# Up's and gate's last 64-row products issued as a pair on the two halves of TensorE's rows, gate's weight stack turned over

## What is computed

```python
up = jax.nn.silu(jnp.einsum('td,edh->teh', xt, Wu) + bu)
gt = jnp.einsum('td,edh->teh', xt, Wg) + bg
act = up * gt * w_full[:, :, None]
y = jnp.einsum('teh,ehd->td', act, Wd) + w_full @ bd
sh = jax.nn.silu(xt @ sWu + sbu) * (xt @ sWg + sbg)
y = y + sh @ sWd + sbd
```

## Time and profile before

| what | value |
|---|---|
| runs | 437.08, 439.56, 439.49 us, median 439.49 |
| profiled execution | 437.12 us, its span 435.3 us |
| granted TensorE clock, mean | 0.998 |
| PE busy | 422.8 us, 97% of the span, 2425 matmuls |
| PEld busy | 358.3 us, 82% |
| DVE busy | 309.1 us, 71% |
| ACT busy | 221.3 us, 51% |
| POOL busy | 99.4 us, 23% |

### The profile page before, as it was taken

How to read it: one execution, slowest core, us unless ns; L and a number is a source line. 1 busy time by engine, 2 the same in 40 slices (tenths; PEclk the granted TensorE clock), 3 DMA queues, 4 the chain that set the end, 5 groups by cost and what they waited for, 6 DMA issues and landing times.

```text
span 435.3 us, 7041 instructions
## 1 busy us (share of the span) xinstructions
PE 422.8 (97%) x2425; PEld 358.3 (82%) x2425; DVE 309.1 (71%) x966; ACT 221.3 (51%) x642; POOL 99.4 (23%) x143
## 2 busy tenths in 40 slices
PE   8999999999999999999999999999999999999995
PEld 7787679877799766997767987887888888889994
DVE  4888865487654796626989659888668688566564
ACT  1667666265672366923661356773444633434432
POOL 4131122132122222120041527985301100000000
PEclk9999999999999999999999999999999999999999
DMA  5979999999999999997650016222043220333300
GB/s 164 310 279 196 208 214 213 214 213 213 213 213 213 214 213 213 211 213 166 246 199 2 1 41 232 80 50 68 5 137 106 68 71 23 105 87 86 86 23 36
DMA packets 20997, 63.60 MB, mean 146 GB/s; under 512 B 2572, under 2 KB 10964, under 8 KB 20578
## 3 DMA queue, kind: packets, MB, share of 16 engines
q0 software_dynamic: 7552, 39.39, 42.9%
q1 hardware_dynamic: 12546, 22.68, 17.5%
q10 hardware_dynamic: 864, 1.09, 0.8%
HBM read 61.88 MB, written 1.27 MB: 145 GB/s over the span
## 4 chain that ended last, share of the span: by engine, by line
PE 51%; DMA 33%; DVE 8%; ACT 4%; issue 2%; SPq 1%; POOL 1%; ACTq 0%; DVEq 0%
DMA area_w<-in_L_attn_wte_dram 27%; PE bank L911 8%; PE bank L995 4%; PE bank L997 4%; PE bank L998 4%; PE bank L996 4%; PE bank L999 4%; DMA area_t<-in_L_attn_W_o_dram 3%; PE bank L1034 2%; PE bank L1043 2%; PE bank L1044 2%; PE bank L1035 2%; PE bank L1036 2%; PE bank L857 2%; DMA lnw<-in_L_attn_ln_w_dram 1%
## 5 line engine op out<-in xcount | busy, mean ns | idle before, releaser
L579 ACT ACTIVATE area_p<-area_p,nmax 128x128 f32<-128x128 f32 x96 | 37.4, 390 | 72.1 <-DVE nmax L1184 72.1
L911 PE MATMUL bank<-area_t,area_o 128*128 128x192 f32 (+1 forms) x432 | 72.3, 327 | 0.0
L911 PEld LDWEIGHTS bank<-area_t,area_o 128*128 128x128 f32 (+1 forms) x432 | 69.8, 182 | 0.6 <-issue 0.6
L650 ACT ACTIVATE area_p_r<-area_b 128x484 fp32r<-128x484 f32 (+1 forms) x51 | 30.6, 601 | 78.0 <-DVE area_b L1295 77.9
L471 POOL DMA_DIRECT2D area_w<-in_L_attn_wte_dram x26 | 31.1, 1196 | 129.2 <-DMA area_w<-in_L_attn_wte_dram 129.2
L857 PE MATMUL bank<-area_p,xn 128*128 128x356 f32 x96 | 39.7, 495 | 0.0
L1281 DVE SCALAR_TENSOR_TENSOR area_b<-bank,area_w 128x484 f32<-128x484 f32 (+1 forms) x36 | 23.4, 650 | 21.5 <-ACT bank L677 16.6
L602 ACT ACTIVATE area_b<-xb,w 64x192 f32<-64x192 f32 x96 | 38.1, 444 | 0.8
L1182 DVE CUSTOM_DVE_ANT_0 area_p<-bank,cmask 128x128 f32<-128x128 f32 x96 | 23.9, 286 | 12.6 <-PE bank L810 12.5
L799 PE MATMUL bank<-area_a,xa 128*128 128x256 f32 x96 | 29.1, 384 | 0.5 <-DVE area_a L1172 0.4
L521 POOL TENSOR_TENSOR area_b_r<-area_b,area_p_r 128x484 fp32r<-128x484 f32 x17 | 21.8, 1280 | 28.6 <-ACT area_p_r L650 28.6
(11 more groups left out here) (269 smaller groups left out, 1059.4 us busy)
## 6 DMA issues: line engine op xcount, KB each, us to landing
area_w<-in_L_attn_wte_dram POOLq DMA_DIRECT2D x28, 1344.0 KB, 12.6
area_w<-gate_rows SPq DMA_DIRECT2D x24, 242.0 KB, 3.2
area_k<-in_experts_dram SPq DMA_DIRECT2D x8, 353.0 KB, 5.8
area_w<-gate_rows SPq DMA_DIRECT2D x12, 228.0 KB, 3.2
area_a<-in_experts_dram SPq DMA_DIRECT2D x6, 353.0 KB, 5.5
area_b<-gate_rows SPq DMA_DIRECT2D x8, 242.0 KB, 3.2
area_t<-in_L_attn_W_o_dram SPq DMA_DIRECT2D x1, 1728.0 KB, 11.1
area_o<-in_x_dram SPq DMA_DIRECT2D x4, 384.0 KB, 6.1
```

The costliest lines, as they stand in the source:

```text
L579: act.activation(pm[:, sl, n, :], pm[:, sl, n, :], ACT.Exp, scale=-1.0, bias=nmax[:, sl, n:n + 1], accum_out=psums[:, sl, n:n + 1])
L650: act.activation(hid_high[:, sl, 0:w], hidT[:, sl, 0:w], ACT.Copy).then_inc(hid_high_ready, 1)
L911: last = pe.matmul(o, oT[:, c, at:at + n], woT[:, c, :], start=(c == 0), stop=(c == NCH - 1))
```

## The change

`products` issues four matmuls and no longer the fifth. A new function `half_rows(n)` is called at the end of `gate_of(n)` and issues two matmuls of 64 rows: up's high weights (rows 0 to 63 of its stack) with rows 0 to 63 of `xbl`, and gate's high weights with rows 64 to 127 of `xbl`. For that gate's stack is turned over: low rest in rows 0 to 63, high part in rows 64 to 127. `upper` and `sign` get a second column for gate, and ACT's and DVE's instruction for the stack becomes two, one for up and one for gate. `up_ready` is now raised by up's half-row matmul, which stands behind gate's four. The product of low weights with low activations of the 64 features is no longer computed (for the other 128 features it never was).

```diff
+            for c in range(2):
+                own.mark(pool.affine_select(out=upper[:, c:c + 1], in_=upper[:, c:c + 1], compare_op=ALU.is_gt, fill=1.0 - c,
...
+                own.mark(pool.affine_select(out=sign[:, c:c + 1], in_=sign[:, c:c + 1], compare_op=ALU.is_gt, fill=2.0 * c - 1.0,
...
-                act.activation(signed, wb(e), ACT.Copy, scale=sign[:, 0:1]).then_inc(wh_ready, 1)
+                act.activation(signed[:, 0], wb(e)[:, 0], ACT.Copy, scale=sign[:, 0:1])
+                act.activation(signed[:, 1], wb(e)[:, 1], ACT.Copy, scale=sign[:, 1:2]).then_inc(wh_ready, 1)
...
                 pe.matmul(o, both, xbh[:, p, 0:w], start=False, stop=False)
-                return pe.matmul(o, both, xbl[:, p, 0:w], start=False, stop=True)
+
+            def half_rows(n):
+
+                sl, g, e = n % 2, n // STEPS, n % STEPS
+                w, p = WIDE[g], g % 2
+                pe.matmul(bank[sl][:, 0:w], wbs(e)[0:64, 0], xbl[0:64, p, 0:w], start=False, stop=True).then_inc(up_ready, 1)
+                pe.matmul(bank[2 + sl][:, 0:w], wbs(e)[64:P, 1], xbl[64:P, p, 0:w], start=False, stop=True).then_inc(gt_ready, 1)
...
-                products(bank[sl], 0, g, e).then_inc(up_ready, 1)
+                products(bank[sl], 0, g, e)
...
-                products(bank[2 + sl], 1, g, e).then_inc(gt_ready, 1)
+                products(bank[2 + sl], 1, g, e)
+                half_rows(n)
...
-                dve.scalar_tensor_tensor(out=wbs(e), in0=wb(e), scalar=upper[:, 0:1],
-                                         in1=turned_sign(e), op0=ALU.mult, op1=ALU.add).then_inc(wbs_ready, 1)
+                for c in range(2):
+                    last = dve.scalar_tensor_tensor(out=wbs(e)[:, c], in0=wb(e)[:, c], scalar=upper[:, c:c + 1],
+                                                    in1=turned_sign(e)[:, c], op0=ALU.mult, op1=ALU.add)
+                last.then_inc(wbs_ready, 1)
```

More of the change, by code:

```diff
@@ L107, in early_fusion_kernel @@
         nnreg = sb("nnreg", [P, 2])
-        upper = sb("upper", [P, 1])
-        sign = sb("sign", [P, 1])
+        upper = sb("upper", [P, 2])
+        sign = sb("sign", [P, 2])
         postab = sb("postab", [P, E])
@@ L417, in _ @@
             own.mark(pool.memset(wrest[:], 0.0))
-            own.mark(pool.memset(upper[:], 0.0))
-            own.mark(pool.memset(sign[:], 1.0))
+            own.mark(pool.memset(sign[:, 0:1], 1.0))
+            own.mark(pool.memset(upper[:, 0:1], 0.0))
+            own.mark(pool.memset(sign[:, 1:2], -1.0))
+            own.mark(pool.memset(upper[:, 1:2], 1.0))
             pool.wait_ge(pool_own, own.at)
@@ L435, in _ @@
             pool.wait_ge(pool_own, own.at)
[L436 to L439, removed]
+            for c in range(2):
+                own.mark(pool.affine_select(out=upper[:, c:c + 1], in_=upper[:, c:c + 1], compare_op=ALU.is_gt, fill=1.0 - c,
+                                            base=64, pattern=[[0, 1]], channel_multiplier=-1))
+                own.mark(pool.affine_select(out=sign[:, c:c + 1], in_=sign[:, c:c + 1], compare_op=ALU.is_gt, fill=2.0 * c - 1.0,
+                                            base=64, pattern=[[0, 1]], channel_multiplier=-1))
             own.mark(pool.memset(mhalf[:], -0.5))
```

## The result

The changed kernel takes 448.36 us (median of 4 runs, 447.61 to 449.78) against 438.28 us (436.82 to 439.56) before. The ratio on record is 1.0244, 95% interval 1.0221 to 1.0267 (the two medians alone give 1.0230): slower. The profiled execution took 448.68 us, its span is 446.9 us, at a mean granted clock of 0.994.

The account below looks back on a forecast made before the run. TensorE's matmul stream was taken as the bound in steady stretches, ACT and DVE's chain in part of group 0. Terms 7.8 + 1.5 + 0.5 + 0.2 + 0.9 = +10.9 us gave 449.0 us, range 440.5 to 454.0.

Parts of the forecast that it names:

- Crossings: Each step's switches into and out of half rows: 0.18 us each, +7.8 us over all steps after the saved pitch.
- Steps 8 to 13: Group 0 around the routing: later `silu` of step 8 and extra stack instructions delay up(13), +1.5 us.
- The length of a stall: Sign in the profile after: TensorE's wait at up(13) in group 0 would grow to nearly 2 us.
- The split in the attention: Last pair of the attention: stack instructions cut in two on DVE and ACT lengthen the chain, +0.9 us.
- The group starts: Two group starts: `summed_out` on ACT stands behind a later `hidden_high`, 0.1 us each, +0.2 us.
- The tail: End of the kernel: later `hidden_low` of step 49 delays the last down matmuls, +0.5 us beyond the step's own growth.
- two starting points: Bases for the sum: the profiled execution, 437.1 us, giving 448.0, and the runs' median 2.4 us above it, giving 450.4.

Follow-up runs that it names:

- e1: Changed kernel with the pair's two matmuls on all 128 rows, same place and order, split stack and late `up_ready` kept; 442.29 us against 437.46, ratio 1.0100.
- e2: Changed kernel without gate's half-row matmul, only up's left; 450.15 us, ratio 1.0276.
- e5: Kernel before with only the stack's instruction split in two on ACT and on DVE, same values; 440.16 us, ratio 1.0063.
- e6: Kernel before with only up's fifth full product moved behind gate's, so `up_ready` is raised late; 440.87 us, ratio 1.0079.
- e10: Changed kernel with up, gate and down all in half rows in steps 17 to 49 only, and one signed copy on ACT; 436.28 us, ratio 0.9974.
- e7: Changed kernel with gate's half of one step paired with up's of the next, behind up's four products, `up_ready` early again; 451.60 us, ratio 1.0328.
- e8: Changed kernel with all up, gate and down products from step 2 on as paired half-row matmuls, 14 pairs a step; 441.58 us, ratio 1.0099.
- e4: Changed kernel without the pair, 13 full matmuls a step, `up_ready` early again; 429.14 us (one run).

## Why the prediction was right

The forecast was 449.0 us and slower; it came to 448.36. Point by point:

- **Crossings, right in mechanism, a little small.** I took 0.18 us for each; the timeline shows 0.19. The step grew by 0.16 us in group 1 and 0.19 in group 2, predicted were 0.149 and 0.160. Over all steps the difference between e1 and the changed kernel is 7.2 us, predicted 7.8: less, because where TensorE waits for DVE anyway a longer step costs nothing. I had the two half-row starts 7 ns apart; they are 3 to 4, and both rows say 354.48. The Trainium skill (TensorE: Matmul & The Clock Gate, Part 3, Measured speedup vs the span model) puts each further packed matmul at about 4 ns; e2 and these rows agree that the second half is as good as free. The Trainium skill (TensorEngine Tiling (Array Packing), Key Properties) has a change of tiling mode drain the engine, and the 51 idle times in front of the pair agree; what a drain costs is what this trace adds.
- **Steps 8 to 13, right in mechanism, one cost missing.** Predicted +1.5 beyond the steps. `silu(8)` starts 2.79 us behind up(8) instead of 1.30, the 1.5 us that I gave it, and from up(8) to up(13) it takes 19.06 us instead of 17.02, 2.04 more, 1.2 beyond five steps' own growth. That the later `silu(8)` and the extra stack instructions add up is borne out by up(13) in e5, e6 and e1. What I didn't have: a part of the split's delay is made in steps 0 to 3, where DVE's normalisation instruction meets POOL's `hidden_low` and takes 1.3 us instead of 0.31. So e5 alone is 1.06 us slower in group 0, where I had 0.8 for four stacks.
- **The length of a stall.** I expected the wait of up(13) near 2 us; the longest is 1.2 in the changed kernel and 1.4 in e1, e5 and e6, where the timeline of before has 0.4 at the same place. Since the step is as long as DVE takes from `weigh(10)` to `weigh(11)`, a longer step of TensorE leaves a shorter wait in it. I took the lateness of the end for the length of the wait.
- **The split in the attention, right.** Predicted +0.9. From the start of the attention's last half-row matmuls (L810, 217.52 us before and L814, 217.82 after) to up(0) it takes 36.5 us before and in e6, which have no split, and 37.4 in the changed kernel and e5. Counted from the last single one of them it is 36.4 in those two and 37.1 to 37.4 in all ten that have the split, 0.75 to 1.0 more. But I had given part of it to ACT's copies: e10 has one copy again and still takes 37.2, so it is DVE's two instructions. In the medians this part drowns in what moves ahead of it.
- **The group starts.** I took 0.1 us each. In the changed kernel steps 19 and 36 are 0.27 and 0.24 us longer than before, 0.16 and 0.19 of that being their own growth. In e1, without crossings, the same two steps are 0.25 and 0.24 us longer, and the two groups lose 0.3 each: at these places crossing and lateness cost little more together than the lateness alone.
- **The tail.** Predicted +0.5 beyond the step's own growth; it is 0.9 us longer in all, 0.7 beyond the growth, and 0.7 in e1 without any crossing.

The sum of the terms from step 0 on was 10.0 us and came to 10.5. With e1 as the dividing line, the crossings were 0.6 us too large (7.2 for 7.8); lateness and split were 1.1 too small: 0.5 in group 0 (2.0 for 1.5), 0.4 at the group starts (0.6 for 0.2), 0.2 in the tail (0.7 for 0.5). Part of the good agreement is errors of opposite sign. And the total of 449.0 was set near the middle between two starting points 2.4 us apart; the median of before is 438.28 us with its fourth run, which with the same sum gives 449.2.

What stays open: that the long instruction on DVE is caused by POOL's is read from the times (all 48 cases in the twelve traces fit), not from a run that moves one of them. How much of group 0's loss would go if the stack stood behind the normalisation wasn't tried either. For e7, that the late `gt_ready` costs the 1.9 us is argued from the place alone.

## What to carry over

Price a packed pair by its visit, not by its rows: here it saves one pitch (0.21 us) and pays two crossings (0.39 us), so it needs two saved pitches for each visit, and it can pay only where many half-row products stand together, as in e8 to e10. When a signal is moved later, ask at each place where the consumer's chain is already the bound (the routing stretch, a group start, the end). There, delays that two changes make on the same chain add up, even where the stall that they leave on TensorE is no longer than with one: measure when the stall ends, not how long it is. Reordering for TensorE's sake brings little in a stage where DVE and ACT set the pace: e4, with two products a step fewer than before, was no faster in group 0. And before an instruction on one of these engines is made longer, look at what the later start of the next one meets.

## What the runs showed of the hardware that I had not expected

- An fp32r matmul of 64 rows crosses just as a float32 one does, in both directions, which the trace of before couldn't show: 0.09 us in which nothing starts and 0.10 us of open weight load going in, and about as much coming out, 0.39 us for both.
- A DVE instruction of 0.31 us (L1264, 128x64) lasted 1.2 to 1.3 us whenever POOL's tensor-tensor instruction began before it or within 0.02 us of its start, and ended 0.05 us behind POOL's; with POOL's start 0.12 us later it stayed at 0.31.
- A long run of half-row products on both halves keeps the full pitch: in e8 two half products every 0.219 us in group 1 and 0.207 in group 2, loads hidden, and the two halves may hold different stages of the work. The timeline of PE in e8, group 1:

```profile
358.78 0.38 PE L1103 MATMUL bank<-area_b_r,area_t_r 64*128 64x484 f32 x1
358.80 0.38 PE L1103 MATMUL bank<-area_p_r,area_k_r 64*128 64x484 f32 x1
359.00 0.38 PE L1107 MATMUL bank<-area_w_r,area_a_r 64*128 64x484 f32 x1
359.02 0.38 PE L1103 MATMUL bank<-area_b_r,area_t_r 64*128 64x484 f32 x1
```

Each half has its own stream (358.78 and 359.00 on the one, 358.80 and 359.02 on the other), and both last 0.38 us, as a full product does.
